# A ring of gathered rows with eight buffers in place of four, in a two-layer mixture-of-experts kernel

## The chip, the cores and the metric

The kernel runs on one core of a Trainium2 chip. The metric is the device time of one execution in microseconds (us), as the median of several runs.

## What is computed

There are 1,024 tokens of 128 channels in 8 batches. Layer one adds to x a routed feed-forward network (two of eight experts a token) over a projection that depends on the batch. Layer two adds an expert-choice network (each expert takes its 256 best tokens) over a gated projection. Layer one's routed part, which the change touches, is this in the reference:

```
logits = jnp.einsum('tc,ec->te', x_flat, router_w)
probs = jax.nn.softmax(logits, axis=-1)
top_w, top_idx = jax.lax.top_k(probs, K)          # K = 2, E = 8
top_w = top_w / (jnp.sum(top_w, axis=-1, keepdims=True) + 1e-09)
h = jnp.einsum('tc,efc->tef', x_flat, w1) + b1[None]
h = jax.nn.relu(h)                                # F = 512
y = jnp.einsum('tef,ecf->tec', h, w2) + b2[None]
sel = jnp.take_along_axis(y, top_idx[:, :, None], axis=1)
out = jnp.einsum('tkc,tk->tc', sel, top_w)
```

## The kernel before

Engines run their own instruction streams and order themselves by semaphores. The work around the change is layer one's routed experts.

The 2 x 1,024 pairs of token and expert are sorted by expert into 16 blocks of 128 rows (NB = 16). The projected tokens stand in the DRAM tensor `rows0`. Block 0 is picked from SBUF by matmuls (`pick_first`, line 581), and blocks 1 to 15 are fetched by 15 indirect DMAs of GpSimd (`gather`, line 454), each of 128 rows of 512 bytes, into the ring `xs` [128, RING, 128]. Block b uses buffer b % RING and the semaphore `gathered[b % RING]`. TensorE turns each block (`turn_x`, line 592), which counts `x_turned` up (the count is b + 1 once block b is turned), and ScalarE copies it to SBUF (`take_x`, line 936).

A gather may overwrite its buffer once the block that was in it has been turned:

```
if b >= RING:
    pool.wait_ge(x_turned, b - RING + 1)
```

Experts are worked off in 23 pairs of a block and an expert (NPAIR = 16 + 8 - 1). For pair j TensorE does the up projection (`up`, line 617, four products with the weights copied to `w1_now` by VectorE, line 1207), ScalarE the bias and Relu (`take_h`, line 952), TensorE the down projection (`down0`, line 627), and VectorE adds the bias row (`bias`, line 1225) and the masked result (`keep`, line 1233) to the block's sum in `y0`, counting `y_kept`. TensorE's order is written out: turn block j, up of pair j-1, down of pair j-2.

After its 15 gathers GpSimd issues 16 scatters (`scatter`, line 459) of the finished blocks to the DRAM tensor `picked`. Scatter b waits for `keep` b + 8. When all have landed, SyncE (line 378) and ScalarE (line 968) load the results in token order (`got`), and layer two begins.

SyncE meanwhile loads the weights of both layers, all at line 378 or 394. The second half of w2 waits until three blocks are turned, and each of the eight groups of layer two's weights waits for one or two further turns (`x_turned`), so that they spread over the stage. No load waits for a gather.

Of the kernel before, what the change touches and what calls it, by code (L numbers as in the profile page):

```python
# [32 lines left out]
H = 256  # L33
K = 2
LORA_SCALE = 32.0 / R
RING = 4
WB_RING = 4
NB = K * T // P
NPAIR = NB + E - 1
# [73 lines left out]
def adaln_moe(nc, xT, x, first, second, rows, w1, w2, cond_w, gate_w, v1, c1, v2, consts, out):  # L113
    with ExitStack() as ctx:
        def sb(name, shape, dt=F32):
            return ctx.enter_context(nc.sbuf_tensor(name, shape, dt))

        def sem(name):
            return ctx.enter_context(nc.semaphore(name))
# [90 lines left out]

        xs = sb("xs", [P, RING, C])
        w1_now = sb("w1_now", [P, WB_RING, FW])
# [96 lines left out]

        gathered = [sem(f"gathered_{q}") for q in range(RING)]  # L310
        h0_ready = sem("h0_ready")
# [126 lines left out]
        def _(pool):  # L438
# [7 lines left out]
            def rows_at(idx, i):  # L446
                return bass.IndirectOffsetOnAxis(ap=idx[:, i:i + 1].bitcast(U32), axis=0)
# [3 lines left out]
            def gather(b):  # L451
                if b >= RING:
                    pool.wait_ge(x_turned, b - RING + 1)
                pool.indirect_dma_start(out=xs[:, b % RING], out_offset=None, in_=rows0,  # L454
                                        in_offset=rows_at(gidx, b)).then_inc(gathered[b % RING], 16)

# [1055 lines left out]
```

## Time and profile before

| | us |
|---|---|
| median of three runs | 163.64 |
| the three runs | 163.5, 163.64, 164.37 |
| span of the profiled execution, first to last instruction | 150.0 |
| median less the span | 13.6 |
| TensorE busy | 138.6 |
| VectorE busy | 94.5 |
| ScalarE busy | 84.9 |
| GpSimd busy | 61.4 |

The span is from one profiled execution, whose own time isn't given apart from the three runs. Busy time is a sum over the whole span; which engine sets the pace has to be read stage by stage. The names in the profile are those of the program: `PE` is TensorE's matmul, `PEld` its weight load, `DVE` VectorE, `ACT` ScalarE, `POOL` GpSimd, `SPq` SyncE's queue. The profile writes `xg` for `xsT`, which shares its memory, `w_sb` for w1 and w2, and `y` for `y0`.

### The profile page before, as it was taken

How to read it: one execution, taken by the hardware profiler on the slowest of the kernel's cores; microseconds unless marked ns; L12 is line 12 of the kernel's file. 1: busy time of each engine (PE TensorE's matmuls, PEld its weight loads, DVE VectorE, ACT ScalarE, POOL GpSimd, SP SyncE). 2: the span in 40 equal slices, each digit the busy share in tenths (PEclk: the TensorE clock that was granted, in tenths of full speed). 3: DMA queues.
4: the chain of work that ended last, by engine and by line, in shares of the span. 5: the costliest groups of instructions: out<-in, count | busy, mean ns of one | idle time of the engine just before them, and what ended most of it. 6: DMA issues, size and time to landing. Idle time of an engine off the chain costs nothing.

```text
span 150.0 us, 3681 instructions
## 1 busy us (share of the span) xinstructions
PE 138.6 (92%) x1139; PEld 122.1 (81%) x1139; DVE 94.5 (63%) x323; ACT 84.9 (57%) x259; POOL 61.4 (41%) x65
## 2 busy tenths in 40 slices
PE   7999887999999999999999997979998999999970
PEld 3765777999999999964789975748988999999960
DVE  5467947555556565452699777767242597748891
ACT  0688826777777666620377769985326255557400
POOL 5000376544477555560500000003677778777000
PEclk9999999999999999999999999999999999999996
DMA  4999614999999991113602940030022222457714
GB/s 142 357 403 315 216 37 89 312 367 393 394 396 342 300 331 37 38 36 88 211 0 116 400 190 0 0 153 2 19 56 50 56 50 59 152 174 236 254 47 140
DMA packets 12965, 26.10 MB, mean 174 GB/s; under 512 B 2082, under 2 KB 5538, under 8 KB 12562
## 3 DMA queue, kind: packets, MB, share of 16 engines
q1 hardware_dynamic: 10336, 21.54, 40.9%
q0 software_dynamic: 1760, 3.67, 8.1%
q10 hardware_dynamic: 850, 0.66, 1.3%
q8 instruction: 10, 0.16, 0.4%
q14 instruction: 9, 0.07, 0.2%
HBM read 19.92 MB, written 5.93 MB: 172 GB/s over the span
## 4 chain that ended last, share of the span: by engine, by line
PE 68%; DVE 14%; DMA 5%; issue 4%; ACT 3%; POOL 3%; DVEq 0%; ACTq 0%
PE bank L617 13%; PE bank L627 13%; PE bank L709 10%; PE bank L818 7%; PE bank L676 3%; PE bank L581 3%; DVE c_tok L1416 2%; POOL xg L476 2%; PE bank L685 2%; DMA got<-picked 2%; PE bank L508 2%; PE bank L770 2%; DMA xg<-rows,idx 2%; DMA picked<-y,sidx 1%; PE bank L543 1%
## 5 line engine op out<-in xcount | busy, mean ns | idle before, releaser
L952 ACT ACTIVATE hT<-bank,w_now 128x128 f32<-128x128 f32 x88 | 25.1, 368 | 11.5 <-PE bank L617 11.5
L1032 ACT ACTIVATE h1T<-bank,c_sb 128x256 f32<-128x256 f32 x44 | 18.3, 471 | 13.7 <-PE bank L709 13.7
L454 POOL DMA_INDIRECT xs<-rows,gidx x15 | 15.1, 1006 | 24.1 <-DVE gidx L1186 14.6
L627 PE MATMUL bank<-w_sb,hT 128*128 (+1 forms) x184 | 24.4, 276 | 0.3 <-ACT hT L952 0.3
L617 PE MATMUL bank<-xg,w_now 128*128 (+1 forms) x176 | 23.4, 276 | 0.8 <-ACT xg L936 0.8
L627 PEld LDWEIGHTS bank<-w_sb,hT 128*128 128x128 f32 x184 | 22.4, 192 | 0.5 <-ACT hT L952 0.5
L617 PEld LDWEIGHTS bank<-xg,w_now 128*128 128x128 f32 x176 | 21.4, 192 | 1.1 <-issue 1.0
L459 POOL DMA_INDIRECT picked<-y,sidx x16 | 15.7, 979 | 10.0 <-DVE y L1233 8.5
L476 POOL DMA_INDIRECT xg<-rows,idx x14 | 14.8, 1054 | 5.0 <-issue 3.7
L1233 DVE SCALAR_TENSOR_TENSOR y<-bank,pairm,y 128x128 f32 (+1 forms) x23 | 8.1, 351 | 10.2 <-PE bank L627 10.0
L709 PE MATMUL bank<-xgT,v_sb 128*128 128x256 f32 x56 | 14.2, 384 | 0.0
L488 POOL TENSOR_TENSOR hlfv<-hlf1h,cst 128x16 bf16<-128x16 bf16 (+1 forms) x2 | 1.3, 692 | 30.6 <-DVE hlf1h L1365 30.6
L1225 DVE SCALAR_TENSOR_TENSOR y<-b_sb,pairm,y (+1 forms) x23 | 8.1, 351 | 8.5 <-issue 7.8
L818 PEld LDWEIGHTS bank<-v_sb,h1T 128*128 128x128 f32 x96 | 11.6, 192 | 0.3
L483 POOL DMA_INDIRECT plane<-x_sb,idx x10 | 10.5, 1049 | 3.0 <-issue 2.1
L818 PE MATMUL bank<-v_sb,h1T 128*128 128x128 f32 x96 | 11.7, 275 | 0.0
L508 PE MATMUL bank<-ones 128*128 128x512 bf16 x41 | 10.6, 416 | 1.1 <-DVE ones L1118 1.1
L1207 DVE COPY w_now<-w_sb 128x516 f32 (+1 forms) x22 | 9.8, 446 | 2.1 <-issue 1.9
L709 PEld LDWEIGHTS bank<-xgT,v_sb 128*128 128x128 f32 x56 | 9.8, 192 | 1.0
L800 PE MATMUL bank<-v_sb,h1T 128*128 128x128 f32 x80 | 10.1, 278 | 0.0
L800 PEld LDWEIGHTS bank<-v_sb,h1T 128*128 128x128 f32 x80 | 9.5, 192 | 0.2
L709 PE MATMUL bank<-w_eff,v_sb 128*128 128x256 f32 x32 | 9.1, 393 | 0.0
(214 smaller groups left out, 246.9 us busy)
## 6 DMA issues: line engine op xcount, KB each, us to landing
v_sb<-in_v SPq DMA_DIRECT2D x16, 256.0 KB
cw_sb<-in_cond_w SPq DMA_DIRECT2D x8, 386.5 KB
plane<-y SPq DMA_DIRECT2D x5, 512.0 KB, 5.1
w_sb<-plane SPq DMA_DIRECT2D x10, 256.0 KB, 3.1
w_sb<-in_w SPq DMA_DIRECT2D x2, 1024.0 KB, 7.6
w_sb<-in_w SPq DMA_DIRECT2D x1, 1290.0 KB, 7.9
w_sb<-in_w SPq DMA_DIRECT2D x1, 774.0 KB, 5.8
rows<-row SPq DMA_DIRECT2D x1, 544.0 KB, 3.3
```

Source lines behind the costliest of these rows:

```text
L454: pool.indirect_dma_start(out=xs[:, b % RING], out_offset=None, in_=rows0, in_offset=rows_at(gidx, b)).then_inc(gathered[b % RING], 16)
L459: pool.indirect_dma_start(out=picked, out_offset=rows_at(sidx, b), in_=y0[:, b], in_offset=None).then_inc(scattered, 16)
L476: pool.indirect_dma_start(out=xg[:, i], out_offset=None, in_=rows1, in_offset=rows_at(idx1, i)).then_inc(gathered1[e], 16)
L483: pool.indirect_dma_start(out=plane[e], out_offset=rows_at(idx1, i), in_=y1[:, e % Y1_RING, h], in_offset=None).then_inc(added[e], 16)
L508: pe.matmul(out_bank[:], ones[:], ones[:].unsqueeze(1).to_broadcast([P, 4, P]), start=True, stop=True)
L617: mm = pe.matmul(bank[2 + j % 2][:, P * f:P * f + P], w1_of[:, P * f:P * f + P], xsT[:, bass.ds((j - e) * P, P)], start=True, stop=True)
L627: mm = pe.matmul(bank[6 + j % 2][:, 0:C], hT[:, j % 2, P * f:P * f + P], w2_sb[:, bass.ds(e * (NF * C) + f * C, C)], start=(f == 0), stop= ...
L709: mm = pe.matmul(bank[UP_BANKS[u % 4]][:, CAP * f:CAP * f + CAP], v1_sb[:, e, P * fc:P * fc + P], rows_in, start=True, stop=True)
L800: mm = pe.matmul(bank[y_bank(n, h)][:, C * h:C * h + C], h1T[:, n % 2, f, P * h:P * h + P], v2_sb[:, e, f], start=(f == 0), stop=(f == NF ...
L818: mm = pe.matmul(bank[y_bank(n, h)][:, C * h:C * h + C], h1T[:, n % 2, f, P * h:P * h + P], v2_sb[:, e, f], start=(f == 0), stop=(f == NF ...
L952: ins = act.activation(hT[:, j % 2, P * f:P * f + P], bank[2 + j % 2][:, P * f:P * f + P], ACT.Relu, bias=w1_of[:, F + f:F + f + 1])
L1032: act.activation(h1T[:, n % 2, fc], bank[UP_BANKS[(2 * n + h) % 4]][:, CAP * f:CAP * f + CAP], ACT.Gelu, bias=c1_sb[:, e * NF + fc:e * NF ...
```

## The change

One constant is doubled. The ring `xs` becomes [128, 8, 128] (2 KB more a partition), there are eight semaphores `gathered` in place of four, and gather b waits for the turn of block b - 8 in place of b - 4. The number, size and order of all transfers and matmuls stay as they are.

```
-RING = 4
+RING = 8
 WB_RING = 4
```

These lines follow from it, unchanged in themselves:

```
xs = sb("xs", [P, RING, C])
gathered = [sem(f"gathered_{q}") for q in range(RING)]
pe.wait_ge(gathered[b % RING], 16 * ((b - 1) // RING) + 16)
```

## Rows read from the trace of the kernel before

**Rows 1.** The page: the span, and TensorE's busy time, share and instructions.
```profile
span 150.0 us, 3681 instructions
...
PE 138.6 (92%) x1139; PEld 122.1 (81%) x1139; DVE 94.5 (63%) x323; ACT 84.9 (57%) x259; POOL 61.4 (41%) x65
```

**Rows 2.** The chain of waits, 30 to 41 us: start, duration, what.
```profile
35.95 0.89 PE bank L627 x8
36.85 0.11 PE bank L592
36.96 0.98 PE bank L617 x8
```

**Rows 3.** The waits, engine TensorE, 22 to 66 us: in total, times, longest.
```profile
PE bank L617 <- ACT xg L936: 0.8, 1, 0.8
PE bank L627 <- ACT hT L952: 0.3, 1, 0.3
```

**Rows 4.** The chain of waits where the stage ends.
```profile
66.11 0.36 DVE y L1233
...
66.73 2.24 DMA picked<-y,sidx
```

**Rows 5.** Timeline of GpSimd: gathers 4, 5, 6, 8, 9, 15; scatters 0, 5.
```profile
22.10 0.95 POOL L454 DMA_INDIRECT xs<-rows,gidx  x1 [0.30 <-issue]
23.35 0.94 POOL L454 DMA_INDIRECT xs<-rows,gidx  x1 [0.30 <-issue]
24.85 0.94 POOL L454 DMA_INDIRECT xs<-rows,gidx  x1 [0.56 <-PE bank L592]
...
27.75 0.94 POOL L454 DMA_INDIRECT xs<-rows,gidx  x1 [0.66 <-PE bank L592]
29.64 0.94 POOL L454 DMA_INDIRECT xs<-rows,gidx  x1 [0.95 <-PE bank L592]
...
41.11 0.94 POOL L454 DMA_INDIRECT xs<-rows,gidx  x1 [0.95 <-PE bank L592]
42.36 1.00 POOL L459 DMA_INDIRECT picked<-y,sidx  x1 [0.30 <-issue]
...
49.05 0.97 POOL L459 DMA_INDIRECT picked<-y,sidx  x1 [0.45 <-DVE y L1233]
```

**Rows 6.** Instructions of line 454: what ended their engine's idle time, us, times.
```profile
  PE bank L592: 8.0, 9
```

**Rows 7.** TensorE, line 592: timeline of block 9; all turns, first and last start.
```profile
36.57 0.14 PEld L592 LDWEIGHTS bank<-ident_sb,xs 128*128 128x128 f32 x1
...
L592 PEld LDWEIGHTS bank<-ident_sb,xs x15: 142/143/144, 22.2 to 48.0; 128*128 128x128 f32 x15
```

**Rows 8.** Line 454, issue to landing: gathers 5, 6, 15, 9 in turn.
```profile
DMA to landing us min/median/max: 2.4/2.4/2.4
...
DMA to landing us min/median/max: 5.2/5.2/5.2
...
DMA to landing us min/median/max: 6.0/6.0/6.0
...
DMA to landing us min/median/max: 6.8/6.8/6.8
```

**Rows 9.** Table by stage: busy us by engine, clock, DMA share, GB/s.
```profile
25.00:36.00 11.00, 11.00 (x101) 11.00 (x100) 6.45 (x18) 8.27 (x31) 6.22 (x7) 1.00 0.96 329
```

**Rows 10.** Late w2: its issue, its landing (line 378), its first use (line 627).
```profile
24.61 0.33 SPq L378 DMA_DIRECT2D w_sb<-in_w  x1
...
DMA to landing us min/median/max: 5.3/5.3/5.3
...
L627 PEld LDWEIGHTS bank<-w_sb,hT x8: 192/192/192, 31.9 to 32.7; 128*128 128x128 f32 x8
```

**Rows 11.** Timeline of VectorE: a copy beside gather 8, and the third `keep`.
```profile
27.74 0.47 DVE L1207 COPY w_now<-w_sb 128x516 f32 x1
...
29.37 0.35 DVE L1233 SCALAR_TENSOR_TENSOR y<-bank,pairm,y 128x128 f32 x1 [0.38 <-PE bank L627]
```

## The prediction

> **What bounds the kernel now.** I read the page first, for the busiest engine. TensorE is busy for 138.6 of the 150.0 us of the span [rows 1], so the question is whether TensorE ever waits for what the edit touches. The edit touches layer one's routed experts, from about 17 to 67 us, where fifteen indirect gathers bring 128 rows each into the ring `xs`. The chain of waits comes second. Through that stage it runs on TensorE alone: eight matmuls of line 617, eight of line 627, one turn of line 592 of a gathered tile, 0.89 + 0.89 + 0.11 = 1.89 us for a pair of block and expert [rows 2]. No gather is in it. The waits of TensorE between 22 and 66 us, read third, say the same: 0.8 us at the first block and 0.3 us at the last one, both for ScalarE, and nothing for a DMA [rows 3]. The stage ends on the last `keep` of VectorE, the last scatter and its landing [rows 4].
>
> Fourth, GpSimd's own order of time. Its first three gathers need no free buffer, then gather b waits until the tile b-4 has been turned. Gathers 4 and 5 still follow the issue rhythm of about 1.25 us (22.10 to 23.35); from gather 8 on they follow TensorE's 1.89 us, and the last one, gather 15, goes out at 41.11 [rows 5]. The view of who waits for whom puts 8.0 us of idle GpSimd over nine gathers down to line 592 [rows 6]. This is the wait that the edit takes away. GpSimd isn't the bound here, so those 8.0 us are no gain by themselves.
>
> **Part 1: gathers start earlier.** With eight buffers gathers 1 to 7 wait for nothing, and gather b from 8 on waits for the turn of tile b-8. Issued one after another at 1.25 us, from 23.35 for gather 5, they would start at 24.60 (6), 25.85 (7), 27.10 (8), 28.35 (9), 29.60 (10), and so on to 23.35 + 10 x 1.25 = 35.85 for gather 15. The strictest remaining wait is that of gather 15 for the turn of tile 7. Tile 9 is loaded for its turn at 36.57 [rows 7], so tile 7 two steps of 1.89 us earlier, at 32.8, before gather 14 starts at 34.60: it holds nothing up. So gather 9 starts 29.64 - 28.35 = 1.3 us earlier and gather 15 starts 41.11 - 35.85 = 5.3 us earlier.
>
> What is that worth to TensorE? Gather 5 takes 2.4 us from issue to landing, while the DMA engines have little else. From gather 6 on the weights of layer two keep them busy: gather 6 takes 5.2 us, gather 9, the slowest of all, 6.8, and gather 15 6.0 [rows 8]. Gather 9 is the closest: 29.64 + 6.8 = 36.44, and TensorE begins to load tile 9 at 36.57 [rows 7]. It is in time by 0.13 us. Gather 15 lands at 41.11 + 6.0 = 47.1, 0.9 us before its turn at 48.0 [rows 7]. So in the profiled execution all fifteen land in time and the gain is 0. The edit can only widen a margin that is already positive. From above, a gain is bounded by how far the chain is off its rhythm: one step of line 617 takes 0.98 in place of 0.89 [rows 2], right after that narrowest turn. I take 0 of these 0.09 us, because the turn itself is not late.
>
> **Part 2: what stands behind the gathers on GpSimd's queue.** The sixteen scatters. Now the first goes out at 42.36, back to back with gather 15, and by the sixth at 49.05 the queue has caught up with VectorE [rows 5]: it waits again for `keep`, which follows TensorE. Scatter b needs `keep` b+8. After the edit GpSimd is free at 36.8, so scatter 0 can go when the eighth `keep` is done: the third starts at 29.37 [rows 11], five steps of 1.89 and its 0.35 us make 39.2. The next four follow at that rhythm, up to 3 us earlier than now. Scatter 5 and all later ones wait for the same `keep` as before. The last starts at 66.73 and lands 2.24 us later [rows 4]; nothing of that moves. Gain 0.
>
> **Part 3: the DMA engines.** The same 15 gathers of 64 KB run, only sooner. Between 25 and 36 us the engines are busy for 0.96 of the time, at 329 GB/s [rows 9]. 64 KB at that rate is 0.2 us. The one load with a deadline in that stretch is the late half of w2: issued at 24.61, landed 5.3 us later, at 29.9, and first used by the down projection that starts at 31.9 [rows 10]. In that window at most one or two more gathers fall than now (0.2 to 0.4 us of traffic), with 2.0 us of margin. Cost 0. If that cover were gone, the 0.4 us would be paid once. The loads of layer two, paced by SyncE on the turns and not on the gathers, keep their times; they aren't used before 72 us. Their sequencer's queue isn't touched.
>
> **Part 4: VectorE beside denser gathers.** Beside gathers the copy of expert weights takes 0.47 us [rows 11]. In each 1.89 us VectorE does one such copy and two operations of 0.35, 1.17 us in all, so it has 0.7 us to spare. With a gather every 1.25 us in place of 1.89 us, there is half a gather more a step. Even if the copy grew by the whole 0.47 once more in a step, it would be 1.64 of 1.89. Cost 0, and it ends at 36.8 in place of 42. The Trainium skill (SBUF — State Buffer, the section SBUF: two separate sides) says that a float32 copy from SBUF to SBUF on VectorE locks GpSimd out while it builds descriptors. By that rule a gather could be held for 0.47 us a time and the rhythm would be 1.72 instead of 1.25 us. The row speaks against it in this kernel: gather 8 started at 27.75 beside a copy and took the same 0.94 us as gathers 5 and 6 [rows 5]. Nor would it matter, since 1.72 is still shorter than TensorE's 1.89.
>
> **Part 5: four more semaphores and 2 KB a partition.** Four are added to the 148 that the code asks for. The time outside the span is 163.64 - 150.0 = 13.6 us. If all of that were in proportion to the number of semaphores, four would cost 13.6 x 4 / 148 = 0.37 us; from below it is 0. I take 0, since nothing in the trace ties this time to their number. The tensors after `xs` move by 2,048 bytes; no row shows an address that matters, and I take 0, with no gain or loss to bound beyond the same 0.37.
>
> **Sum.** Gathers 0 (bounds -0.09 to 0), scatters 0, DMA 0 (to +0.4), VectorE 0, semaphores 0 (to +0.37). The profiled span stays 150.0 us. The times of the three runs are 13.6 us above it at the median, and I keep that part: 150.0 + 13.6 = 163.6 us. A difference under 0.5%, 0.82 us, can't be told from none.
>
> **Rivals.**
>
> *Faster: the margin of 0.13 us is not there in every execution.* For it speaks how narrow it is, and that the three times lie 0.87 us apart. Were landings 1 us slower than profiled (7.8 us), gather 9 would come 0.87 us late. A late turn delays the next gathers too, so with four buffers the delay settles at about 7.8 us for four steps instead of the 6.93 from issue to load: 0.22 us a step over some four steps, again 0.9 us. Eight buffers would win that back: 163.64 - 0.9 = 162.7 us. Against it: gather 9 is the slowest of the fifteen, gather 15 has 0.9 us to spare, and the profiled execution pays none of it. A part of this, 0.2 or 0.3 us, would stay inside "same".
>
> *Slower: gathers in flight share their bandwidth.* Now a gather of 6.8 us overlaps 6.8 / 1.89 = 3.6 gathers. At a distance of 1.25 us it is 5.4. If all in flight progressed together at the present total rate, gather 9 would take 6.8 x 5.4 / 3.6 = 10.2 us, land at 28.35 + 10.2 = 38.55 and hold TensorE for 2.0 us: 165.6 us. It decides from an issue-to-landing time for gather 9 of 8.2 us (36.57 - 28.35) on, and it shows in the time from 9.0 on. For it: gathers 6 to 9 were issued 4.8 us apart from first to last and landed 6.4 us apart (24.85 + 5.2 = 30.05 to 36.44), 2.1 us each [rows 5, 8], so something does ration them. Against it: this is equally what a queue served in order gives. Served in order, a gather that stands in line behind the same predecessors, all issued no later than now, lands no later than now; the time from issue to landing only grows by the earlier issue. The Trainium skill (DMA: Bandwidth & Descriptors, Queues, rings and completion order) says that each DMA engine takes its queues in turn, a packet at a time, and each ring's descriptors in order. By that rule the earlier gathers aren't slowed by later ones, and the trace, with its landings in order, agrees; what it would slow is the w2 load of part 3.
>
> *The edit does what it says but shows nowhere.* That is the forecast. That it does nothing at all is excluded: nine waits of 8.0 us are in the trace.
>
> **How the numbers follow.** No change 0.86; the faster rival in full, or the setup getting shorter, 0.08; the slower rival 0.06. The likeliest is 163.6 us. Both rivals' tails are small, so the range is that of no change: down to 162.9, most of the way to the faster rival's 162.7, and up to 163.64 + 0.37 + 0.4 = 164.4, the upper bounds of the semaphores and of w2.
>
> **What would show it.** In the new profile gather 15 should start near 35.9 and not at 41.1, GpSimd's idle time behind line 592 fall from 8.0 us to about nothing, the first scatter come at about 39.4 (0.1 after its `keep`) and the sixth still at about 49.05. The chain should still be TensorE's 1.89 us steps, with the last scatter near 66.7, and the span 150.0. Gather 9 should land between 35.2 (6.8 us after its issue) and 36.4, its issue-to-landing time up to 8.1. I am wrong if TensorE waits for `xs` at line 592 (slower rival), if the first turns or the stage's end shift, or if the span stays and the time moves (semaphores).

## The result, and the profile after

Four executions of the changed kernel took 166.34 to 166.91 us, median 166.74. The kernel before took 164.0 in that comparison (median of four). The measured ratio is 1.0248, with a 95% interval of 1.0191 to 1.0305: slower by 1.9 to 3.1%. The medians themselves lie closer, 2.7 us or 1.7% apart (3.1 us or 1.9% if the one execution of 168.1 us among the four is left out), so the size is less sure than the direction. I had forecast 163.6 us and no change. Some executions of either kernel come out several us longer than the rest; the ratios leave those out.

The page of the changed kernel stands beside [rows 1]. The third row is the granted clock in 40 slices of the span, in tenths.

```profile
span 164.5 us, 3681 instructions
...
PE 146.0 (89%) x1139; PEld 127.6 (78%) x1139; DVE 93.9 (57%) x323; ACT 85.4 (52%) x259; POOL 61.7 (37%) x65
...
PEclk9999999956999999999999999999997599999997
```

The execution took 166.34 us, so the time outside its span is 1.8 us. In the prediction that part was 13.6 us. Both can't be a fixed cost of the same launch. The span of 150.0 us that I read must be that of an execution of about 152 us, and the three times of 163.5 to 164.37 us belong to executions that I had not seen. The later runs bear this out: time less span is 1.8 to 1.9 us in each of their executions.

The chain of waits of the changed kernel in the stage of the edit, beside [rows 2]:

```profile
27.23 0.89 PE bank L627 x8
28.13 0.11 PE bank L592
28.24 5.61 issue
33.85 2.07 PE bank L617 x8
35.92 1.71 PE bank L627 x8
```

TensorE stands still for 5.61 us, and then works at half its rate (1.71 us for eight matmuls in place of 0.89). The table by stage gives the granted clock, third from the right: 0.50 from 34 to 40 us, which is the lower of its two levels, 1.2 GHz. In the 6 us before, TensorE had been busy for 0.39 us.

```profile
28.00:34.00 6.00, 0.39 (x4) 0.16 (x1) 0.69 (x2) 0.83 (x4) 3.28 (x4) 0.93 0.97 344
34.00:40.00 6.00, 6.00 (x29) 6.00 (x30) 2.42 (x7) 2.76 (x11) 2.41 (x3) 0.50 0.74 239
```

Who is late? In the timeline of all engines around the hole, the turn of block 3 begins at 26.07 us and that of block 4 at 27.96. GpSimd goes on issuing gathers. Three engines wait for TensorE's signals and start again within a quarter of a us of one another. `<-remote` says that the wait ended with a signal for which the profile finds no instruction that ended just before it.

```profile
26.07 0.27 PE L592 MATMUL bank<-ident_sb,xs 128*128 128x128 f32 x1
...
27.86 0.94 POOL L454 DMA_INDIRECT xs<-rows,gidx  x1 [0.30 <-issue]
...
27.96 0.27 PE L592 MATMUL bank<-ident_sb,xs 128*128 128x128 f32 x1
...
30.35 0.94 POOL L454 DMA_INDIRECT xs<-rows,gidx  x1 [0.30 <-issue]
...
33.17 0.37 ACT L936 ACTIVATE xg<-bank,first_sb 128x128 f32<-128x128 f32 x1 [6.39 <-remote]
33.22 0.35 DVE L1233 SCALAR_TENSOR_TENSOR y<-bank,pairm,y 128x128 f32<-128x128 f32 x1 [7.15 <-remote]
33.41 0.94 POOL L454 DMA_INDIRECT xs<-rows,gidx  x1 [2.11 <-remote]
```

ScalarE's copy of block 3 needs the turn of block 3 and its own operation before, both done by 26.8 us, and it starts at 33.17. VectorE's `keep` needs a down projection that ended at 26.24, and starts at 33.22. Gather 11 needs the turn of block 3 and starts at 33.41. TensorE in turn waits for ScalarE's copy, so it stops too. No transfer of `xs` is in this chain. A second such hole is in layer two, where VectorE waits 4.9 us from 122 us on.

What the trace holds of the signals themselves fits signals that arrive late: TensorE ended a down projection at 26.24, an up at 27.23, a down at 28.13 and a turn at 28.23 us, yet between 26.79 and 33.11 us there is no record of an engine raising a semaphore; the next one of `x_turned` is at 33.15. (Such records can be missing at this level, as said below.) And it isn't TensorE's signals alone. SyncE needs no new signal for its load at 33.05 us (it waits for three turned blocks, and had them at 25.37). In between it works on small instructions of its own registers that wait for nothing. One kind of them, with shortest, median and longest duration in ns, first in the changed kernel, then in the kernel before:

```profile
L394 SPq SEQ_ASSERT  x2: 112/406/700, 26.5 to 30.9; - x2
...
L394 SPq SEQ_ASSERT  x4: 18/18/29, 25.8 to 32.5; - x4
```

So several engines are held up, SyncE's own small steps too, until near 33.1 us.

### The profile page after: what moved, and what is told of

Its sections match the earlier page's. It is cut to its first block, busy times and chain, and to the rows that moved or that the text cites. A ratio compares the mean times of both kernels' runs of the same rounds, so it can differ in the third digit from the quotient of the medians.

```text
span 164.5 us, 3681 instructions
## 1 busy us (share of the span) xinstructions
PE 146.0 (89%) x1139; PEld 127.6 (78%) x1139; DVE 93.9 (57%) x323; ACT 85.4 (52%) x259; POOL 61.7 (37%) x65
## 4 chain that ended last, share of the span: by engine, by line
PE 62%; DVE 13%; issue 9%; ACT 5%; DMA 4%; another core or an unknown queue 3%; ACTq 0%; POOL 0%; DVEq 0%
PE bank L617 13%; PE bank L627 13%; PE bank L818 7%; PE bank L709 7%; PE bank L800 3%; DVE c_tok L1416 3%; PE bank L770 2%; DMA got<-picked 2%; PE bank L676 2%; PE bank L685 2%; PE bank L518 2%; PE bank L508 2%; DMA picked<-y,sidx 1%; PE bank L543 1%
## 5 line engine op out<-in xcount | busy, mean ns | idle before, releaser
L617 PE MATMUL bank<-xg,w_now 128*128 (+1 forms) x176 | 25.2, 290 | 6.4 <-issue 5.6
L617 PEld LDWEIGHTS bank<-xg,w_now 128*128 128x128 f32 x176 | 23.1, 204 | 6.9 <-issue 6.9
L627 PE MATMUL bank<-w_sb,hT 128*128 (+1 forms) x184 | 25.6, 284 | 0.3 <-ACT hT L952 0.3
L627 PEld LDWEIGHTS bank<-w_sb,hT 128*128 128x128 f32 x184 | 23.6, 201 | 0.5 <-ACT hT L952 0.5
L709 PE MATMUL bank<-xgT,v_sb 128*128 128x256 f32 x56 | 15.4, 405 | 1.7 <-issue 1.7
L818 PEld LDWEIGHTS bank<-v_sb,h1T 128*128 128x128 f32 x96 | 13.2, 215 | 0.7 <-issue 0.3
L818 PE MATMUL bank<-v_sb,h1T 128*128 128x128 f32 x96 | 13.6, 300 | 0.1
L709 PEld LDWEIGHTS bank<-xgT,v_sb 128*128 128x128 f32 x56 | 10.3, 201 | 3.2 <-issue 2.2
L936 ACT ACTIVATE xg<-bank,first_sb 128x128 f32<-128x128 f32 x16 | 6.0, 377 | 10.4 <-remote 6.4
L1207 DVE COPY w_now<-w_sb 128x516 f32 (+1 forms) x22 | 9.3, 425 | 2.1 <-issue 1.8
L800 PE MATMUL bank<-v_sb,h1T 128*128 128x128 f32 x80 | 10.1, 278 | 0.0
L800 PEld LDWEIGHTS bank<-v_sb,h1T 128*128 128x128 f32 x80 | 9.5, 192 | 0.2
```

Source lines behind the costliest of these rows:

```text
L617: mm = pe.matmul(bank[2 + j % 2][:, P * f:P * f + P], w1_of[:, P * f:P * f + P], xsT[:, bass.ds((j - e) * P, P)], start=True, stop=True)
L627: mm = pe.matmul(bank[6 + j % 2][:, 0:C], hT[:, j % 2, P * f:P * f + P], w2_sb[:, bass.ds(e * (NF * C) + f * C, C)], start=(f == 0), stop= ...
L709: mm = pe.matmul(bank[UP_BANKS[u % 4]][:, CAP * f:CAP * f + CAP], v1_sb[:, e, P * fc:P * fc + P], rows_in, start=True, stop=True)
L800: mm = pe.matmul(bank[y_bank(n, h)][:, C * h:C * h + C], h1T[:, n % 2, f, P * h:P * h + P], v2_sb[:, e, f], start=(f == 0), stop=(f == NF ...
L818: mm = pe.matmul(bank[y_bank(n, h)][:, C * h:C * h + C], h1T[:, n % 2, f, P * h:P * h + P], v2_sb[:, e, f], start=(f == 0), stop=(f == NF ...
```

## The experiments

Eighteen runs come in six groups. Each group ran on one chip, with the kernel before beside it. The six groups fell on five chips: those of `n2` and `n3` are on the same one.

### The same two kernels again, and the buffers without the earlier gathers

`a_before` and `a_after` are the two kernels unchanged. `b_buffers_only` has the eight buffers and semaphores, and the old waits:

```
-RING = 4
+RING = 8
+LEAD = 4
...
-if b >= RING:
-    pool.wait_ge(x_turned, b - RING + 1)
+if b >= LEAD:
+    pool.wait_ge(x_turned, b - LEAD + 1)
```

`c_ring6` has RING = 6.

> The kernel before, once more, for a second profile. Theory A (the 5.6 us hole of TensorE near 28 us in the changed kernel is a disturbance that executions of both kernels have, and the first profile of before happened to be free of it): the time is 163.6 us and the span about 1.8 us below the time, near 162, with one or more holes of TensorE of several us. Theory B (the hole is made by the earlier gathers): the span is again near 150 us, 13.6 us below the time, and TensorE waits 1.1 us between 22 and 66 us.

> The changed kernel once more. Theory A: the holes lie elsewhere or have other lengths than in the first profile (5.6 us near 28, 4.9 us near 122). Theory B: the hole near 28 us is there again, 5 to 6 us long, and the time is 166.3 to 166.9 us.

> Eight buffers and semaphores, but gather b still waits for the turn of block b-4. Theory B (earlier gathers cost the time): 163.6 us, as before, with gathers at TensorE's rhythm. Rival C (the four semaphores or the moved addresses cost it): 166.7 us, with gathers at the old rhythm. Theory A: anything between, by the holes that the execution has.

> Six buffers and semaphores. Theory B: gathers 6 and 7 go out at once, later ones two steps earlier than with four; between 163.6 and 166.7 us. Rival C: half of the added semaphores, about 165.2 us. Theory A: no ordering by the number of buffers.

Here the kernel before took 152.82 us. The profile of `a_before` has a span of 149.9 us at a time of 151.72. `b_buffers_only` came to a ratio of 0.9985 (0.994 to 1.0029) and `c_ring6` to 0.9989 (0.9948 to 1.0029). `a_before` and `a_after` have too few executions for a ratio; the profiled one of `a_after` took 152.85 us, with no hole near 28 us. So there are two levels that don't come from the kernel: 152 us, to which the profile that I had read belongs, and 164 us, that of the first comparison. Later groups fell on one or the other whole, so the level goes with the chip or the hour; no chip on record was met at both.

### The two kernels once more, and other numbers of buffers

`n_before` and `n_after` are again the two kernels, `d_ring12` has RING = 12 and `e_ring3` has RING = 3.

> The kernel before against itself, to see how large a difference the comparison finds between equal kernels. Theory A (the 2.5% belong to the chip and moment of that comparison, not to the kernel): a ratio within 0.5% of 1 where the executions are undisturbed, and no better agreement here than in the run of the changed kernel beside it. Theory D (a disturbed chip punishes the earlier gathers): ratio 1.00 here whatever the level.

> The changed kernel. Theory A: ratio 0.995 to 1.005 on a chip at the 152 us level; on one at the 164 us level a ratio no further from 1 than that of the kernel before against itself. Theory D: 1.00 at the 152 us level, but 1.02 to 1.03 at the 164 us level. My first reckoning (earlier gathers are free): gather 15 starts near 36 us, no wait of TensorE for xs.

> Twelve buffers: gathers 1 to 11 wait for nothing, the last one starts near 36 us as with eight, since GpSimd's own 1.25 us sets the pace. Theory A: ratio 1.00 to before. Theory D or B: as n_after or slower.

> Three buffers: gather b waits for the turn of block b-3, so from its issue to its turn there are three steps less 0.65 us, 3 x 1.89 - 0.65 = 5.0 us, against the 5.2 to 6.8 us that gathers 6 to 15 took. If the lead matters as I read it, TensorE waits for xs: each step becomes (landing time + 0.65) / 3, so 2.2 us at a landing time of 6.0, for ten steps 3 us more: near 155 us at the 152 us level. If landing times shrink with fewer gathers in flight (shared bandwidth: three in place of 3.6), less than 1 us.

| | ratio to before | 95% interval |
|---|---|---|
| n_before | 0.9972 | 0.9935 to 1.0008 |
| n_after | 1.0011 | 0.9976 to 1.0046 |
| d_ring12 | 1.0032 | 1.0 to 1.0063 |
| e_ring3 | 1.0199 | 1.0104 to 1.0294 |

The changed kernel is as fast as the one before. Three buffers cost 2.0% (from three executions), 3.0 us of 152.8, as reckoned from the landing times. In the profiled execution of `e_ring3`, from the first matmul of line 617 (24.77) to the last scatter (72.11), the stage takes 47.34 us, 4.0 more than the 43.33 that it takes with four or eight buffers. The waits of TensorE from 22 to 70 us, beside [rows 3], now begin with the gathers:

```profile
PE bank L592 <- DMA xs<-rows,gidx: 1.6, 3, 0.7
```

The chain of `e_ring3` goes through a whole gather, from its issue (34.27) over its landing to its turn:

```profile
34.27 6.29 DMA xs<-rows,gidx
40.55 0.04 issue
40.60 0.33 PE bank L592
```

So the lead of a gather does matter: three steps are too short and four are just enough. In `d_ring12` gather 9 took 6.5 us from issue to landing, with about five gathers in flight, against 6.8 [rows 8] with fewer than four. More gathers in flight didn't lengthen it.

### Loads that don't wait for turns, with four and eight buffers

To lengthen the landing times, SyncE's loads of layer two's weights lost their waits for turns:

```
 for e in range(E):
-    sp.wait_ge(x_turned, 2 * e + 1)
     load_cond(e)
-    sp.wait_ge(x_turned, 2 * e + 2)
     load(v1_sb[:, e], v1[:, e * F:(e + 1) * F], in_v)
```

> Four buffers; SyncE no longer waits for turns between the groups of layer two's weights (16 loads of v and 8 of cw go out in one train from about 26 us). The DMA engines were already at 0.96 to 1.04 busy from 25 to 49 us, so if the gathers' landing time is set by queueing behind that traffic it stays at 6 to 7 us and the time stays at 152 to 153 us. If a deeper queue of loads lengthens it, gather 9's margin of 0.13 us is gone and TensorE waits for xs at line 592: up to 1 us a turn for landing times of 10 us ((10 + 0.65) / 4 - 1.89 = 0.8 us), some 3 to 6 us in all.

> The same with eight buffers. If landing times stay, the same time as f_flood4. If they lengthen to 10 us, the earlier issue (1.3 us for gather 9, up to 5.3 for gather 15) covers most of it, and f_flood8 is 1 to 5 us faster than f_flood4. Shared bandwidth (my slower rival) would make it slower than f_flood4.

> The kernel before against itself again. Wanted: an execution at the 164 us level with a profile. Theory A: if this comparison meets such a level, this profile has holes in which TensorE's signals reach ScalarE, VectorE and GpSimd some 5 us late, as the first profile of the changed kernel has near 28 and 122 us, 5 and more us each, somewhere. Theory E (such holes come only where GpSimd issues indirect gathers back to back): at that level the kernel before has the hole of layer two's gathers, near 110 us, and none near 28 us. At the 152 us level neither says anything.

> The changed kernel. Theory A: ratio to before within 0.5% of 1 at the 152 us level. Theory E: the same there, but 2 to 3% slower at the 164 us level, with one hole more than the kernel before, near 28 us.

Measured were 0.9997 (0.9962 to 1.0032) for `f_flood4` and 1.0014 (0.9968 to 1.0059) for `f_flood8`; `n2_before` 0.9974 (0.9931 to 1.0017) and `n2_after` 0.9986 (0.9949 to 1.0024). The flood was a weak one. The eight groups of loads still start some 2.3 us apart (34.24, 36.72, 38.86 us for three in a row), from the first to the last in 16.1 us, where the kernel before with its waits takes 21.7 (26.00 to 47.68). The gathers of `f_flood4` land in 6.5 us at the most, those of `f_flood8` in 6.9. So the landing times didn't grow, and this pair says nothing on longer ones.

The timeline of GpSimd in `n2_after`, beside [rows 5], is what the prediction said of the order of work (gathers 1, 9, 15, scatters 0, 5 and 15):

```profile
18.03 1.83 POOL L454 DMA_INDIRECT xs<-rows,gidx  x1 [15.21 <-DVE gidx L1186]
...
28.92 0.95 POOL L454 DMA_INDIRECT xs<-rows,gidx  x1 [0.30 <-issue]
...
36.43 0.95 POOL L454 DMA_INDIRECT xs<-rows,gidx  x1 [0.30 <-issue]
40.56 1.00 POOL L459 DMA_INDIRECT picked<-y,sidx  x1 [3.18 <-DVE y L1233]
...
49.53 0.97 POOL L459 DMA_INDIRECT picked<-y,sidx  x1 [0.92 <-DVE y L1233]
...
67.22 0.97 POOL L459 DMA_INDIRECT picked<-y,sidx  x1 [0.53 <-DVE y L1233]
```

Its first gather is 0.57 us later than before (17.46 us there). Less that, gather 15 starts at 35.86, the first scatter at 39.99, the sixth at 48.96 and the last at 66.65.

### The 164 us level

> The kernel before against itself. Theory A and theory E: ratio 1 at either level. At the 164 us level its profile shows whether the hole near 28 us, seen in the changed kernel, is there too (A) or not (E).

> The changed kernel. Theory A: ratio within 0.5% of 1 at the 152 us level, and within the spread of before against itself at the 164 us level. Theory E: 1.02 to 1.03 at the 164 us level.

> Eight buffers, gathers at the old times. Theory A: as before. Theory E: as before at the 164 us level too, and 2 to 3% faster than the changed kernel there.

The level was 152 us again: 1.0017 (0.9974 to 1.006) for `n3_before`, 0.9966 (0.9931 to 1.0001) for `n3_after`, 0.9992 (0.995 to 1.0033) for `n3_buffers_only`. In `n3_after` gather 9 is issued at 29.41, lands 6.6 us later, at 36.01, and is turned at 37.62: the margin of 0.13 us has become 1.6 us and is worth nothing. The instructions of line 454 in it, beside [rows 6]:

```profile
  PE bank L592: 0.6, 2
```

> The kernel before against itself. At the 152 us level a ratio within 0.5% of 1. At the 164 us level its profile says whether it has the hole near 28 us too (theory A) or only ones elsewhere (theory E).

> The changed kernel. Theory A: within 0.5% of 1 at the 152 us level, no further off than before against itself at the 164 us level. Theory E: 1.02 to 1.03 at the 164 us level.

This group met the 164 us level: the kernel before took 163.8 us (median), the changed kernel 165.76. The ratio is 1.0166, 1.0088 to 1.0243. `n4_before` has no ratio; its median is 165.27 us over six executions, from 161.41 to 168.55. So the first result is met a second time at this level, in direction, with less certainty than the interval suggests: the kernel before against itself lies 0.9% apart here by its medians, and over all executions of this group the medians are 163.83 us (17 of the kernel before) and 165.76 (7 of the changed one), 1.2% apart. The profiled execution of `n4_after` took 169.65 us, 3.9 above its median; it is used only for what the first profile of the changed kernel shows as well.

The chain of `n4_after` has the hole of the first profile, at the same place and length:

```profile
28.33 5.57 issue
33.90 2.07 PE bank L617 x8
35.97 1.33 PE bank L627 x8
```

and its timeline the same three engines let go together:

```profile
33.22 0.37 ACT L936 ACTIVATE xg<-bank,first_sb 128x128 f32<-128x128 f32 x1 [6.35 <-remote]
33.26 0.35 DVE L1233 SCALAR_TENSOR_TENSOR y<-bank,pairm,y 128x128 f32<-128x128 f32 x1 [7.10 <-remote]
33.45 0.94 POOL L454 DMA_INDIRECT xs<-rows,gidx  x1 [2.07 <-remote]
```

The kernel before has holes too, but not this one. In the timeline of `n4_before`, first near 27 us, where GpSimd had issued six gathers one after another and gather 7 must wait for a turn; then near 46 us, where the scatters go out back to back behind the last gathers:

```profile
27.11 0.37 ACT L936 ACTIVATE xg<-bank,first_sb 128x128 f32<-128x128 f32 x1 [0.82 <-PE bank L592]
...
27.34 0.95 POOL L454 DMA_INDIRECT xs<-rows,gidx  x1 [1.27 <-PE bank L592]
...
45.19 1.15 POOL L459 DMA_INDIRECT picked<-y,sidx  x1 [0.30 <-issue]
...
46.64 0.97 POOL L459 DMA_INDIRECT picked<-y,sidx  x1 [0.30 <-issue]
48.39 1.14 ACT L952 ACTIVATE hT<-bank,w_now 128x128 f32<-128x128 f32 x4 [2.57 <-PE bank L617]
...
48.91 0.35 DVE L1233 SCALAR_TENSOR_TENSOR y<-bank,pairm,y 128x128 f32 x1 [2.66 <-remote]
```

and in layer two, where gathers follow one another from 110 us, in both kernels the same. Here VectorE waits for slots that TensorE had added up by 118.1, and the DMA engines are busy for only 0.20 of the time from 110 to 122 us, so a hole needs no full DMA engines:

```profile
119.54 0.94 POOL L476 DMA_INDIRECT xg<-rows,idx  x1 [0.30 <-issue]
...
121.96 0.16 DVE L1116 TENSOR_REDUCE idx<-bank 128x2 int32<-128x4 f32 x1 [4.95 <-remote]
```

The stage of the edit can be measured in each profile from the first matmul of line 617 to the start of the last scatter:

| profile | level, us | from | to | length, us |
|---|---|---|---|---|
| before | 152 | 23.31 | 66.73 | 43.42 |
| n2_after | 152 | 23.89 | 67.22 | 43.33 |
| n3_before | 152 | 24.42 | 67.75 | 43.33 |
| n3_after | 152 | 24.36 | 67.69 | 43.33 |
| n4_before | 164 | 23.59 | 71.15 | 47.56 |
| n4_after | 164 | 24.17 | 74.73 | 50.56 |
| after | 164 | 24.08 | 76.25 | 52.17 |

At the 152 us level the stage is as long in both kernels to 0.1 us. At the 164 us level it is 4.1 us longer for the kernel before and 7.1 to 8.8 for the changed one. These sums come out of the holes. In `n4_before` the turns around the first hole are 5.0 us apart in place of two steps of 1.89, those around the second 4.8 in place of one: 1.2 + 2.9 = 4.1 us. In `after` the hole of 5.6 us is followed by 6.8 us at half the clock, which cost 3.4 more; in `n4_after` by 3.4 us at half the clock, which cost 1.7: 9.0 and 7.3 us. The 3.0 us between `n4_before` and `n4_after` are about what the ratio says, 0.0166 x 163.8 = 2.7 us; between `n4_before` and `after` they are 4.6. What follows the stage is longer at this level too, but in both kernels alike: 88.85 us in `n4_before` and 88.25 in `after`, against 83.27 in `before`. (In `n4_after`, the long execution, it is 93.17.)

> Eight buffers and semaphores with gathers at the old times. At the 164 us level: theory E (the train of gathers makes the hole) gives a ratio of 1.00 to before, no hole of 5.6 us near 28 us, and 47.6 us from the first up projection of line 617 to the last scatter, as before; rival C (the semaphores or addresses do it) gives 1.017 and 50.6 us. At the 152 us level it says nothing new: ratio 1.00 and 43.4 us by either.

`n5_buffers_only` fell on the 152 us level, at a ratio of 1.0006 (0.9973 to 1.004). So the buffers without the earlier gathers are free there, in three runs; at the 164 us level they weren't measured.

## Why the prediction was wrong

**The step that failed is part 1's term, "Gathers 0 (bounds -0.09 to 0)",** which left no room for a cost. At the 164 us level, the one of the comparison, the stage that holds the gathers is 3.0 us longer with the change (50.56 against 47.56 us), and 4.6 in the first profile (52.17), by a hole of 5.6 us and the slow clock behind it. That the gathers' pace makes the hole is argued below and not shown; part 5's term for the semaphores (0 to 0.37 us) wasn't measured at this level, so it isn't cleared there.

**The sum hid it.** It put 13.6 us "outside the span" and kept them. They are 1.8 us, and the other 11.8 were work and holes of executions that the profile did not show. This didn't put the base off: 150.0 + 13.6 is the time of before by construction. But the profile and the times were of two levels, and the argument about waits was made on a trace without any hole. A time that lies 13.6 us above its span should have been the first row to explain. Part 5's bound of 0.37 us, a share of the 13.6, falls with it.

**Part 1, its cost.** "The edit can only widen a margin that is already positive" is right for the transfer, as far as the 152 us level shows it; the profiles of the 164 us level give no landing times. It says nothing of what issues the transfer. With four buffers the waits for turns pace GpSimd at 1.89 us from gather 8 on [rows 5]. With eight it issues at 1.25 us through to gather 10 without a pause. At the 164 us level TensorE's partners wait about a us near 27 us in the first case and 6 to 7 us up to 33 in the second. No rival of mine had this: the slower one was about the DMA engines' bandwidth.

**Part 1, the order of work,** was right. At the 152 us level gather 15 starts where it was expected (35.86 against 35.85 us, less the later start), the idle time behind line 592 falls from 8.0 to 0.6 us, and gather 9 lands 1.6 us before its turn.

**Part 2** was right: the sixth scatter at 48.96 against 49.05, the last at 66.65 against 66.7. The first came at 39.99, 0.6 us later than forecast: its `keep` ended at 39.20 as reckoned, but the scatter starts 0.8 us after it and not 0.1. At the 164 us level the scatters have a side that I missed: the kernel before has a hole of 2.4 us where they go out in a row, and in the profiles of the changed kernel, whose scatters wait for `keep`, there is none at that place.

**Parts 3 and 4** held at the 152 us level: TensorE's waits there are those of [rows 3], and the stage keeps its 43.3 us. **Part 5,** the semaphores and the 2 KB, cost nothing there, by `b_buffers_only`, `n3_buffers_only` and `n5_buffers_only` (0.9985, 0.9992, 1.0006).

**The rivals.** The faster one assumed that landings are late in the timed executions. Neither level shows a wait of TensorE for `xs` with four buffers; `e_ring3` shows that the reckoning of leads behind it was sound. The slower one, shared bandwidth, fell at the 152 us level: gather 9 takes 6.5 us with twelve buffers and 6.6 with eight, not 10.2. That agrees with what the Trainium skill says (DMA: Bandwidth & Descriptors, Queues, rings and completion order) of rings worked off in order.

**What is shown and what is argued.** Shown: at the 152 us level there is no difference. At the 164 us level the changed kernel is slower in two comparisons, by 1.7 and 2.5%. Both of its profiles have a hole of 5.6 us at 28 us, and the one profile of the kernel before at this level has smaller ones at other places. In the hole, three engines go on 6 to 7 us after TensorE's work for them ended, together, and SyncE, which waits for no signal there, crawls as well. Argued: that the train of indirect gathers causes it. For that speaks the place of the holes. In the profiles at that level they lie where GpSimd issues in a row: gathers 1 to 10, the gathers and scatters near 45 us, the gathers of layer two. They end 0.8 to 1.9 us after it pauses: at 33.2 us after 31.3, at 48.4 after 47.6, at 122.0 after 120.5. (The pauses near 31 and 120 us come of the hole itself: the next gather waits for a signal that is held.) Against theory A, holes by chance, speaks that the hole came back at the same place to 0.1 us. Rival C, the added semaphores, is excluded at the 152 us level only.

One more rival stands untested: that the recording of the trace, or a path that it shares, is what gets stuck. The three traces of the 164 us level hold 1,992 to 2,121 records of semaphore updates, and the seventeen of the 152 us level 2,861 to 2,882, with 3,680 or 3,681 instructions in each; small instructions of SyncE that wait for nothing and take 0.7 us are in those three alone. Every time in the later groups comes with a span, so with a record; no execution without one is there to compare. By this rival the level and the loss could be a matter of measuring. What differs between the two levels, and what holds the engines up, stays open. Whether spaced gathers with eight buffers are as fast as the kernel before at the 164 us level wasn't measured.

## What to carry to other kernels

Before reading a profile for a change, set its span beside the times: if the two don't lie a fixed small amount apart, the profile is of another kind of execution, and its margins and its missing holes prove nothing about the timed ones. A wait for a free buffer can be more than a wait: it also paces the queue behind it. Deepening the ring when no one waits for its data bought nothing here, and at one of two levels it came with a loss; the number of steps from issue to use (three too few, four enough) says how many buffers are worth having.

## What the runs showed of the hardware

- The same kernel is met at two levels 7% apart: 152.5 to 152.8 us in five groups of runs on four chips, 163.8 us in one on a fifth and 164.0 in the first comparison, with the same time outside the span (1.8 to 1.9 us).
- At the slower level ScalarE, VectorE and GpSimd can go on 2.5 to 7 us after TensorE's work for them has ended, all at once, near runs of indirect DMAs issued 1.25 us apart. SyncE is slow in the same stretch, without a wait: its load of layer two's weights for the second batch starts at 33.05 us, 3.6 us after the issue before it ended at 29.5 (0.8 us in the first profile of the kernel before), and a small instruction of its own takes 0.70 us in place of 0.02. At the other level the same run of gathers does nothing of the kind.
- A hole of 5.6 us costs more than itself: after it TensorE's granted clock is 0.50 for 6.8 us in one profile and 3.4 us in the other, and eight matmuls take 1.71 us in place of 0.89.
- Beside a full load of weights a gather takes 5 to 7 us from issue to landing (once 7.8, with six buffers), with fewer than four of them in flight (6.8 us for gather 9 with four buffers) as with five (6.5 us with twelve), at the 152 us level.
